# Two expert products moved behind the output projection, one normalization moved ahead of their sums, and a second slot for values in DRAM, in a fused attention and expert layer

## What is computed

```python
def attn(x):                      # per token: 16 heads of 16
    xn = ln(x, ln1)
    q, k, v = (xn @ w + b for w, b in (q, k, v))
    fq, fk = elu(q) + 1, elu(k) + 1
    kv = einsum('bhnd,bhne->bnde', fk, v)          # over heads, per token
    num = einsum('bhnd,bnde->bhne', fq, kv)
    den = einsum('bhnd,bnd->bhn', fq, fk.sum(heads)) + 1e-6
    x = x + (num / den) @ wo + bo
    return x + gelu(ln(x, ln2) @ fc_w + fc_b) @ proj_w + proj_b

def experts(x):                   # 8 experts, two chosen per sequence
    logits = x.mean(tokens) @ gate_w.T + gate_b
    gates = softmax(top 2 of logits)
    return sum(gates[e] * gelu(x @ expert_w[e].T + expert_b[e]))

x = x + attn(layernorm(x))
x = x + experts(layernorm(x))
```

## Time and profile before

| | us |
|---|---|
| median of 3 runs | 1277.56 (1273.89 to 1277.82) |
| the profiled execution, its time | 1278.0 |
| its span, first to last instruction | 1276.2 |
| TensorE busy | 1108.7, 87% of the span |
| VectorE busy | 782.9, 61% |
| ScalarE busy | 530.4, 42% |
| mean granted clock of TensorE | 0.884 of full speed |

### The profile page before, as it was taken

How to read it: one execution, slowest core, us unless ns; L and a number is a source line. 1 busy time by engine, 2 the same in 40 slices (tenths; PEclk the granted TensorE clock), 3 DMA queues, 4 the chain that set the end, 5 groups by cost and what they waited for, 6 DMA issues and landing times.

```text
span 1276.2 us, 22032 instructions
## 1 busy us (share of the span) xinstructions
PE 1108.7 (87%) x7272; PEld 816.2 (64%) x7272; DVE 782.9 (61%) x1692; ACT 530.4 (42%) x835; POOL 190.8 (15%) x113
## 2 busy tenths in 40 slices
PE   6646988979797989999997989999999989795946
PEld 3444766757575858686775758586767667583723
DVE  2465566565757586666756676766666674646333
ACT  2413443534444444536353454536363444231322
POOL 1011202020111212120301112121203012111000
PEclk9757897979797989989897989899897989797969
DMA  4966656383737475665737473656658374311013
GB/s 161 187 143 157 116 140 149 104 180 95 173 98 173 104 165 115 173 148 153 168 121 173 114 172 116 160 128 173 148 147 174 125 165 106 102 55 53 17 66 116
DMA packets 242518, 170.21 MB, mean 133 GB/s; under 512 B 177040, under 2 KB 218256, under 8 KB 240144
## 3 DMA queue, kind: packets, MB, share of 16 engines
q1 hardware_dynamic: 235792, 158.80, 52.3%
q10 hardware_dynamic: 6656, 10.50, 2.4%
HBM read 93.75 MB, written 75.50 MB: 133 GB/s over the span
## 4 chain that ended last, share of the span: by engine, by line
PE 48%; issue 23%; DVE 14%; ACT 7%; DMA 3%; SPq 2%; POOL 1%; DVEq 1%; ACTq 0%; POOLq 0%
PE pq L963 13%; PE pj L949 10%; PE ps L925 7%; PE pq L869 5%; PE pt L934 4%; PE pt L857 3%; DVE nd L727 2%; DVE acc L818 2%; DVE am L700 1%; DVE hn L631 1%; ACT am L513 1%; DVE stat L621 1%; DMA scratch_nd<-ot 1%; DMA ot<-scratch_v 1%; SPq L366 1%
## 5 line engine op out<-in xcount | busy, mean ns | idle before, releaser
L716 DVE TENSOR_TENSOR hidden<-xhT,hidden 128x512 fp32r<-128x512 f32 x128 | 96.6, 755 | 224.0 <-ACT hidden L541 224.0
L963 PE MATMUL pq<-hT,w_fc 128*128 128x512 f32 x768 | 225.4, 433 | 9.4 <-DVE hT L723 5.2
L540 ACT ACTIVATE xhT<-pq,col 128x512 f32<-128x512 f32 x128 | 88.0, 688 | 323.1 <-PE pq L963 322.9
L949 PE MATMUL pj<-w_pj,hidden 128*128 128x256 f32 x1536 | 214.1, 288 | 0.7 <-DVE hidden L716 0.7
L949 PEld LDWEIGHTS pj<-w_pj,hidden 128*128 128x128 f32 x1536 | 191.6, 189 | 18.6 <-issue 9.8
L925 PE MATMUL ps<-kq 48*128 48x128 f32 x1024 | 155.7, 436 | 24.0 <-DVE am L700 14.7
L963 PEld LDWEIGHTS pq<-hT,w_fc 128*128 128x128 f32 x768 | 149.0, 207 | 41.3 <-issue 7.7
L700 DVE TENSOR_TENSOR am<-ps,mask 128x512 f32<-128x512 f32 x256 | 164.1, 682 | 17.4 <-PE ps L925 17.1
L925 PEld LDWEIGHTS ps<-kq 48*128 48x128 f32 x1024 | 133.8, 329 | 61.1 <-issue 36.9
L869 PE MATMUL pq<-zT,w_e 128*128 (+1 forms) x256 | 119.4, 614 | 11.8 <-DMA b_e<-in_eb 7.3
L458 POOL TENSOR_TENSOR rs<-var,mhalf 128x4 f32<-128x4 f32 x16 | 18.1, 1132 | 571.2 <-DVE var L744 571.2
(11 more groups left out here) (117 smaller groups left out, 1399.3 us busy)
## 6 DMA issues: line engine op xcount, KB each, us to landing
kq<-scratch_q SPq DMA_DIRECT2D x192, 128.0 KB, 3.7
kq<-scratch_k SPq DMA_DIRECT2D x192, 128.0 KB, 4.5
scratch_q<-hidden SPq DMA_DIRECT2D x32, 512.0 KB, 4.6
scratch_k<-hidden SPq DMA_DIRECT2D x32, 512.0 KB, 6.1
scratch_nd<-ot SPq DMA_DIRECT2D x16, 1024.0 KB, 3.9
nd<-scratch_nd SPq DMA_DIRECT2D x48, 256.0 KB, 3.3
x_sb<-in_x SPq DMA_DIRECT2D x16, 512.0 KB, 4.7
scratch_v<-feat_v ACTq DMA_DIRECT2D x16, 512.0 KB, 2.8
```

The source lines that it names most:

```text
L540: nc.scalar.activation(gelub[:, u], pq[u][:, :], ACT.Gelu, bias=b_fc[:, m:m + 1])
L716: nc.vector.tensor_tensor(hidden[:, m % SLOTS, 1], gelub[:, u], hidden[:, m % SLOTS, 0].bitcast(f32), ALU.subtract).then_inc(S["rest_ready ...
L949: last = nc.tensor.matmul(pj[u][:, D * s:D * (s + 1)], hidden[:, m % SLOTS, a, lo:lo + P], w_pj[:, b, m], start=False, stop=end)
L963: last = nc.tensor.matmul(pq[m % 2][:, :], w_fc[:, b, c, P * m:P * (m + 1)], hT[:, a, c], start=(n == 0), stop=(n == len(order) - 1))
```

## The change

Three edits. In both lists `F1` moves from its place ahead of `A2` (in FULL ahead of `N` and `D2` too) to behind `R`, and `F3` and `FX` stand behind `R` too; so the output projection comes ahead of both experts on TensorE, and the normalization `R` ahead of their sums on VectorE. `VT` and `F2` stay behind them. `scratch_v` gets two slots, by the parity of the tile, and ScalarE's wait for `v_in` ahead of the store goes. ScalarE waits for `q_out` and `k_out` in D2 instead.

```diff
-FULL = ["L", "XS", "M1", "K0", "J2", "Y", "M2", "DS", "M3", "Z", "D1", "M4", "VL", "XL", "X", "E", "J7", "F1", "N", "D2", "K1", "A2", "F3",
-        "FX", "R", "VT", "F2", "B0", "H", "B9", "JA"]
-HEAD = ["L", "XS", "M1", "K0", "J2", "Y", "M2", "DS", "M3", "Z", "D1", "M4", "VL", "XL", "E", "X", "J7", "G", "N", "D2", "K1", "F1", "A2",
-        "F3", "FX", "R", "VT", "F2", "B0", "H", "B9", "JA"]
+FULL = ["L", "XS", "M1", "K0", "J2", "Y", "M2", "DS", "M3", "Z", "D1", "M4", "VL", "XL", "X", "E", "J7", "N", "D2", "K1", "A2",
+        "R", "F1", "F3", "FX", "VT", "F2", "B0", "H", "B9", "JA"]
+HEAD = ["L", "XS", "M1", "K0", "J2", "Y", "M2", "DS", "M3", "Z", "D1", "M4", "VL", "XL", "E", "X", "J7", "G", "N", "D2", "K1", "A2",
+        "R", "F1", "F3", "FX", "VT", "F2", "B0", "H", "B9", "JA"]
...
-        v_dram = nc.dram_tensor("scratch_v", (D, T), f32, kind="Internal").ap()
+        v_dram = nc.dram_tensor("scratch_v", (2, D, T), f32, kind="Internal").ap()
...
-                        src = v_dram.rearrange("(h d) (j b t) -> j b d h t", d=HD, j=NQ, b=2)
+                        src = v_dram[p.t % 2].rearrange("(h d) (j b t) -> j b d h t", d=HD, j=NQ, b=2)
...
-                    wait("v_in", at("v_in"))
                     for m in range(NC):
                         wait(f"pq_free{m}", at(f"pq_free{m}", 1))
-                    act.dma_start(v_dram.rearrange("(c p) t -> p c t", p=P), feat_v[:, :, :]).then_inc(S["v_out"], 16)
+                    act.dma_start(v_dram[p.t % 2].rearrange("(c p) t -> p c t", p=P), feat_v[:, :, :]).then_inc(S["v_out"], 16)
 
                     wait("am_used", at("am_used"))
+                    wait("q_out", at("q_out"))
+                    wait("k_out", at("k_out"))
```

## The result

The changed kernel takes 1319.66 us (median of 4 runs, 1317.54 to 1321.28) against 1277.69 us before (4 runs, 1273.89 to 1278.27): a ratio of 1.0334, 95% interval 1.0306 to 1.0362. It is 42 us slower. The forecast was slower by 25, with a range up to 1318.

A forecast was written before the change was run, and what follows sets the result against it. Behind A2, one VectorE queue races TensorE's remaining work and would hold F2. FULL 17.1, HEAD 1.8 and the iterations without D2 6.4 sum to 25.3 us on 1278.0, giving 1303 us; range 1281 to 1318.

The forecast's parts named there:

- The rival without a wait: Ahead of F2: VectorE's chain is short enough that TensorE goes on without waiting; faster, 1264 us; chance 0.08.
- the rival without contention: At R on VectorE: R escapes GpSimd's addition and takes 1.37 us; no change, 1281 us; chance 0.09.
- N's start: VectorE's N, waiting for the transfer of `nd`, starts 3.32 us after D2's start in FULL iterations.
- Then come F1's two scalings, 1.06, and F3's two sums, 1.54: VectorE's steps behind R, ahead of F2: scalings 1.06 us, sums 1.54 us, F2 starting 0.16 behind them.
- F2's length: TensorE ahead of H: F2 and B0 together take 2.67 us, 1.45 to B0's start and 1.22.
- Six FULL iterations: H starts at 29.43 us against 26.58 from J7's end: +2.85 in each, +17.1 in all.
- The first two HEAD iterations: H starts 29.05 us behind D2's first matmul against 28.45: +0.6 in each of three HEAD iterations, +1.8.
- what stands still loses nothing by it: TensorE's clock at the longer wait ahead of F2: already at the 1.2 GHz level there, so costed at nothing.
- its rival: Behind TensorE's longer stand, the low clock lasts 3.1 us longer in nine iterations: +14, 1317 us; chance 0.17.
- From the last HEAD iteration's D2 on: End of the span: +0.6 us in that HEAD iteration and +6.4 in the two iterations without D2.
- the two iterations without D2: F1 now stands behind A2 and VectorE is again last, so H starts later: +3.2 us each, +6.4.

The follow-up runs named there:

- Filled: The changed kernel with eight dead matmuls on TensorE between VT and F2, into free banks: 1295.7 us, ratio 1.0151 to the kernel before.
- a second mend: The changed kernel with GpSimd's addition to `x_sb` waiting for R and also no `acc_ready` wait in ScalarE's second expert: 1290.9 us, ratio 1.0095.
- the late addition: The kernel before, with GpSimd's addition to `x_sb` made to wait until R is done: 1253.0 us, ratio 0.9804.

## Why the prediction was right or wrong

**Right: the sign, the place and the mechanism.** TensorE waits ahead of F2 for a VectorE chain that has taken in R, GpSimd's power and F1's scalings; TensorE's wait ahead of H is gone; R takes 3.41 (3.39 forecast), with 1.12 idle ahead. The rival without a wait and the rival without contention are out. The slot brought 1.1 to 1.3 us in each HEAD iteration (one slot against two in the new order), and D2 ends there 15.7 behind its start, as forecast.

**N's start.** Forecast 3.32 behind D2's start, measured 3.35 to 3.86 in FULL, 0.3 more on average. It hangs on the arrival of `nd`, and that varies: in the trace before, the third, fourth and fifth iteration have 4.16, 4.22 and 3.96, and the prediction took the sixth, with 3.32 the earliest. Why it varies was not tried.

**The step that failed: "Then come F1's two scalings, 1.06, and F3's two sums, 1.54".** The two were put back to back. Between them stands ScalarE: its F3 waits for `acc_ready`, which F1's scalings raise. In the old order those scalings were long done. In the new one ScalarE's first Gelu of F3 comes behind them: 1.02 us idle on VectorE, and R's end and the sums' start are 1.8 apart instead of 1.06. The wait stands in the code that F1 and F3 share; the prediction priced ScalarE's table and bank there but not this. Without it the kernel took 1298.9, 20.8 less.

This wait is 0.8 of the 1.5 us by which H in FULL came later than forecast (30.9 against 29.43). N's start is 0.3. The last 0.4 is F2's length: the forecast took F2 and B0 at 2.67 from the earlier trace rows and the clock at nothing, but there F2's transposes take 1.52, since the clock fell only within them (at 822.4); in the new order all of F2 runs at 1.2 GHz (1.96), and F2 to H is 3.04. Six FULL iterations bring 25.9 in place of 17.1. The first two HEAD iterations bring 3.6 in place of 1.2 (H 30.1 both times, against 29.05).

**The clock.** The second term that failed is the clock's, put at nothing because "what stands still loses nothing by it". That was half of the truth, and its rival was given 0.17. Behind H the changed kernel lost 5 us over eight iterations, against the kernel before. Filled, the same chain is 24 us shorter. From the seventh to the fourteenth iteration the low stretch lasts 13.7 or 17.1 us in six (23.9 and 10.2 in the other two), where it lasted 10.2 in six and 13.7 in two. The rival's 1317 lies nearest to the measured time, but in part by luck: of its 14 us, 5 are found behind H and 3 in F2's length, and the rest of what the forecast lacked is the wait in F3 and N. From the last HEAD iteration's D2 on, the changed kernel takes 7.5 us longer (forecast 7.0).

Together 29.5 (H, seventh to fourteenth iteration), 5.4 (behind H), 7.5 (from the last HEAD on) and 0.8 ahead of iteration 7 make the 43 between the two spans. The forecast had 25, of which 18 stand against the 29.5. That 7.0 came out as 7.5 is in part luck: the two iterations without D2 brought 2.5 and 2.7 of their 3.2 each, and the other 2.3 are small differences from the last HEAD iteration to the end of the span, of which the forecast had 0.6.

## What to carry to other kernels

When a stage is moved in a hand-written order, follow every wait of every engine in it, also those that have never been seen to wait: a guard that was free becomes a link of the chain when its releaser moves behind something slow. A large addition on GpSimd beside VectorE's instructions on SBUF is to be placed where VectorE has nothing on the critical chain; one added semaphore wait was worth 2% in the kernel before (ratio 0.9804). In the changed kernel the same wait moved the addition onto the next instructions of the chain, and a second mend then brought nothing more. And a wait of TensorE is to be priced with what comes behind it: if it takes the clock down, the dense work that follows pays again.

## What the runs showed of the hardware that was not expected

- Filling TensorE's wait with dead matmuls made the changed kernel 24 us faster (1319.7 to 1295.7), with the half-clock time falling from 348 to 206 us.
- What a chain gives up can come back nearly twice: 20.8 us for 10 us of earlier H in nine iterations (F3's wait), with 8 more behind H, where the low stretches were shorter. It need not: the late addition in the kernel before gave 14 us of earlier H from the seventh iteration on, and 0.5 behind H in eight iterations.
- VectorE's sum of two SBUF tiles, 0.75 us alone, took 2.7 when it began 0.53 behind GpSimd's addition, and ended 0.55 behind that addition's end. The Trainium skill (SBUF — State Buffer, section Who interferes with whom) states that a VectorE instruction with two SBUF inputs contends with a GpSimd instruction that reads SBUF, and that the shared pair is an exclusive lock. The trace agrees to 0.2 us: had nothing of the sum been done under the addition, it would have ended 0.75 behind.
- The switch of ScalarE's table cost 1.30 us from the load's start to the next activation in 25 of the changed kernel's 30 loads (in the other five the activation waited for another engine), and 23 of the loads began within 0.02 us of the activation before; so no trace here shows the drain that the Trainium skill (ScalarE: Activation LUTs, section What ACT_TABLE_LOAD costs) adds.
